# Weights' sums and subtractions at the start of a CIN tower: one operand from PSUM in place of two from SBUF

## The reference

```python
e = stack([tbl_f[ids[:, f]] for f in range(64)], axis=1)        # (512, 64, 16)
x, outs = e, []
for W, b in ((W0, b0), (W1, b1), (W2, b2)):                     # 128 outputs each
    z = einsum('bhd,bfd->bhfd', x, e).reshape(B, h * f, d)      # outer product of the fields
    x = einsum('oc,bcd->bod', W, z) + b[None, :, None]
    outs.append(x.sum(axis=2))
h = concatenate([concatenate(outs, axis=1), dense_ctx], axis=1)  # (512, 400)
y = relu(relu(h @ W_top1 + b_top1) @ W_top2 + b_top2) @ W_top3   # (512, 1)
```

## Time and profile before

| | |
|---|---|
| runs | 1191.19, 1192.84, 1193.23 us, median 1192.84 |
| profiled execution | 1193.48 us, of which the span 1191.7 us |
| PE busy | 1120.7 us (94%) |
| DVE busy | 1011.0 us (85%) |
| POOL busy | 989.1 us (83%) |
| ACT busy | 704.5 us (59%) |
| first matmul | at 49.06 us |

### The profile page before, as it was taken

The page is one execution under the profiler, slowest core; times in us unless marked ns, Lnnn a source line. Parts: engine busy times, 40 slices in busy tenths (PEclk is TensorE's granted clock), DMA queues, the critical chain, the costliest instruction groups (busy, mean ns, idle before and its releaser), DMA issues.

```text
span 1191.7 us, 13969 instructions
## 1 busy us (share of the span) xinstructions
PE 1120.7 (94%) x4212; PEld 758.3 (64%) x4212; DVE 1011.0 (85%) x685; ACT 704.5 (59%) x682; POOL 989.1 (83%) x419
## 2 busy tenths in 40 slices
PE   0379999999999999999999999999999999999998
PEld 0146666666666666666766666666666666667685
DVE  4478998989989999989898998999898889897542
ACT  2245566566666666675666666656666666665533
POOL 6669999999999999999999999999999997776000
PEclk9989999999999999999999999999999999999999
DMA  6552232525252515334252524252342525242991
GB/s 226 137 161 65 85 83 78 161 65 166 73 150 63 155 46 147 91 88 150 64 165 73 156 78 133 68 144 71 111 127 76 154 73 160 76 151 106 273 297 48
DMA packets 103835, 142.85 MB, mean 120 GB/s; under 512 B 11745, under 2 KB 55009, under 8 KB 103042
## 3 DMA queue, kind: packets, MB, share of 16 engines
q1 hardware_dynamic: 95618, 140.42, 39.1%
q0 software_dynamic: 8192, 2.11, 2.0%
HBM read 114.96 MB, written 27.53 MB: 120 GB/s over the span
## 4 chain that ended last, share of the span: by engine, by line
POOL 62%; PE 17%; issue 14%; DMA 4%; DVE 1%; SPq 1%; ACT 1%; POOLq 0%; ACTq 0%; DVEq 0%
POOL z_lo L509 46%; POOL emb L500 16%; PE acc L1015 9%; PE acc L1010 3%; DMA z<-gram_scratch 3%; PE turn_gram_ps L1079 1%; DMA land<-x_scratch 1%; PE z_ps L1141 1%; ACT z_hi L977 0%; DVE z_lo L754 0%; DVE z L577 0%; SPq L441 0%; SPq L369 0%; PE x0t_ps L1183 0%; PE turn_gram_ps L1183 0%
## 5 line engine op out<-in xcount | busy, mean ns | idle before, releaser
L509 POOL TENSOR_TENSOR z_lo<-z,z_hi 128x2048 fp32r<-128x2048 f32 x159 | 734.9, 4622 | 47.0 <-ACT z_hi L789 44.1
L1015 PE MATMUL acc<-z_hi,w_hi 128*128 128x512 f32 x960 | 412.4, 430 | 3.0 <-POOL z_lo L509 2.1
L789 ACT ACTIVATE z_hi<-z 128x2048 fp32r<-128x2048 f32 x160 | 306.3, 1914 | 181.4 <-PE acc L1015 170.4
L1015 PE MATMUL acc<-z_hi,w_lo 128*128 128x512 f32 x960 | 378.8, 395 | 0.0
L1015 PE MATMUL acc<-z_lo,w_hi 128*128 128x512 f32 x960 | 378.8, 395 | 0.0
L577 DVE TENSOR_TENSOR z<-operand_even,x_shift 128x2048 f32<-128x2048 f32 x144 | 328.5, 2282 | 31.8 <-DMA x_shift<-x_scratch 16.8
L500 POOL DMA_INDIRECT emb<-in_tables,rows_chunk x256 | 254.0, 992 | 62.0 <-issue 56.9
L1010 PE MATMUL acc<-z,w_sb 128*128 128x512 f32 x640 | 293.7, 602 | 0.6 <-ACT x L818 0.4
L589 DVE TENSOR_TENSOR z_lo<-z_ps,z_hi 128x1024 fp32r<-128x1024 f32 x160 | 194.5, 1215 | 71.0 <-ACT z_hi L798 71.0
L1015 PEld LDWEIGHTS acc<-z_hi,w_hi 128*128 128x128 f32 x960 | 180.8, 188 | 62.8 <-issue 18.9
L577 DVE TENSOR_TENSOR z<-operand_odd,x_shift 128x2048 f32<-128x2048 f32 x96 | 218.8, 2279 | 0.5 <-ACT operand_odd L765 0.3
(11 more groups left out here) (92 smaller groups left out, 454.2 us busy)
## 6 DMA issues: line engine op xcount, KB each, us to landing
land<-x_scratch SPq DMA_DIRECT2D x128, 256.0 KB
land<-x_scratch SPq DMA_DIRECT2D x128, 128.0 KB
x_shift<-x_scratch SPq DMA_DIRECT2D x16, 1024.0 KB, 5.8
gram_scratch<-gram SPq DMA_DIRECT2D x32, 512.0 KB, 4.3
x_shift<-x_scratch SPq DMA_DIRECT2D x16, 768.0 KB, 7.7
z<-gram_scratch SPq DMA_DIRECT2D x10, 1024.0 KB, 10.8
x_scratch<-emb SPq DMA_DIRECT2D x32, 192.0 KB, 2.9
x_shift<-gram_scratch SPq DMA_DIRECT2D x6, 1024.0 KB, 10.5
```

The costliest lines, as they stand in the source:

```text
L509: pool.tensor_tensor(z_lo[:, slot], z[:, Z_SLOT[pos]], z_hi[:, slot].bitcast(F32), ALU.subtract).then_inc(subtracted, 1)
L789: act.activation(z_hi[:, SPLIT_SLOT[pos]], z[:, Z_SLOT[pos]], ACT.Copy).then_inc(rounded, 1)
L1015: mm = pe.matmul(acc[:, :], w[:, tile, :], zz[:, slot, q, :], start=False, stop=stop and n == 2)
```

## The change

The layer 1 weights are added in pieces of 512 columns. ScalarE first copies each piece of the b half to a PSUM bank; VectorE adds the a half from SBUF and leaves the sum in the bank (split units) or writes it to `w0_sb` (plain unit). ScalarE rounds the pieces from the bank to w_hi, and VectorE subtracts w_hi (SBUF) from the bank (PSUM) to get w_lo. The 48 tiles of layer 2 go the same way in twelve pieces: ScalarE copies a piece to a bank and rounds it from SBUF, VectorE subtracts. Five banks are used in turn: two of z_ps, acc2, turn_gram_ps and x0t_ps. The waits of TensorE are for the last piece.

```diff
--- before.py
+++ after.py
@@ -73,6 +73,14 @@
 GRAM_BLOCKS = 2 * HALF_BLOCKS
 PLAIN_BLOCKS = W2_PART // F_BLOCK
 TOP1, TOP2 = 512, 256
+PIECE = COLS // HID
+L1_PIECES, SPLIT_PIECES = L1_SPLIT // PIECE, SPLIT_TILES // PIECE
+PLAIN_PIECES = (slice(0, COLS), slice(COLS, (L1_PLAIN + 1) * HID))
+
+
+def piece(weights, k):
+
+    return weights[:, k * PIECE:(k + 1) * PIECE, :].rearrange("p t o -> p (t o)")
 
 
 def is_plain(k):
@@ -212,6 +220,7 @@
         ids_sb = ids_sb.bitcast(I32)
         z_flat = z[:, :, :, :].rearrange("p a q n -> p (a q n)")
         w0b_split_stage = z_flat[:, 0:L1_SPLIT * HID].rearrange("p (t o) -> p t o", o=HID)
+        w0b_split_flat = z_flat[:, 0:L1_SPLIT * HID]
         w0b_stage = z_flat[:, L1_SPLIT * HID:(L1_SPLIT + L1_PLAIN + 1) * HID]
 
         wt1_sb, wt1d_sb = x0_shift[:, 0, 0:3, :], x0_shift[0:DENSE, 0, 3, :]
@@ -236,6 +245,12 @@
         z_ps = ps("z_ps", [P, 2, COLS])
         turn_gram_ps = ps("turn_gram_ps", [P, COLS])
         x0t_ps = ps("x0t_ps", [P, 2 * BLOCKS, FIELDS])
+        def stage_of(k):
+
+            return stage[k if k < L1_PIECES else (k - L1_PIECES) % len(stage)]
+
+        stage = [z_ps[:, 0, :], z_ps[:, 1, :], acc2[:, :], turn_gram_ps[:, :],
+                 x0t_ps[:, :, :].rearrange("p b f -> p (b f)")]
 
 
         ids_in, const_in, w0_in, w1_in, w1_split_in, top_in = (sem(s) for s in ("ids_in", "const_in", "w0_in", "w1_in", "w1_split_in", "top_in"))
@@ -244,6 +259,7 @@
         w2_rounded, w2_split = sem("w2_rounded"), sem("w2_split")
         gram_rounded, gram_split = sem("gram_rounded"), sem("gram_split")
         w_rounded, w_split = sem("w_rounded"), sem("w_split")
+        w0_staged = sem("w0_staged")
         rows_step, rows_ready, rows_free, rows_copied, gather_begun = (
             sem(s) for s in ("rows_step", "rows_ready", "rows_free", "rows_copied", "gather_begun"))
         w0_summed = sem("w0_summed")
@@ -546,22 +562,20 @@
                 dve.wait_ge(rows_step, step + 3)
                 dve.tensor_scalar(rows[:, cols], ids_tmp[:, cols], info_sb[:, 2:3], None, ALU.add).then_inc(rows_ready, 1)
 
-            dve.wait_ge(w0_in, 64)
             w0_flat = w0_sb[:, :, :].rearrange("p t o -> p (t o)")
-            dve.tensor_tensor(w_whole[:, 0:L1_SPLIT, :], w_whole[:, 0:L1_SPLIT, :], w0b_split_stage, ALU.add).then_inc(w0_summed, 1)
-            dve.tensor_tensor(w0_flat, w0_flat, w0b_stage, ALU.add).then_inc(w0_summed, 1)
-
-            def split_weights(step, tiles):
-
-                dve.wait_ge(w_rounded, step)
-                dve.tensor_tensor(w_lo[:, tiles, :], w_whole[:, tiles, :], w_hi[:, tiles, :].bitcast(F32),
+            for k in range(L1_PIECES):
+                dve.wait_ge(w0_staged, k + 1)
+                dve.tensor_tensor(stage[k], piece(w_whole, k), stage[k], ALU.add).then_inc(w0_summed, 1)
+            for k, cols in enumerate(PLAIN_PIECES):
+                bank = stage[L1_PIECES + k][:, 0:cols.stop - cols.start]
+                dve.wait_ge(w0_staged, L1_PIECES + k + 1)
+                dve.tensor_tensor(w0_flat[:, cols], w0_flat[:, cols], bank, ALU.add).then_inc(w0_summed, 1)
+            for k in range(SPLIT_PIECES):
+                dve.wait_ge(w_rounded, k + 1)
+                dve.tensor_tensor(piece(w_lo, k), stage_of(k), piece(w_hi, k).bitcast(F32),
                                   ALU.subtract).then_inc(w_split, 1)
-
-            split_weights(1, slice(0, L1_SPLIT))
-            split_weights(2, slice(L1_SPLIT, SPLIT_TILES))
             dve.wait_ge(const_in, 48)
             dve.tensor_scalar(bias3_sb[:, :], bias_sb[:, 2:3], float(EMBED), None, ALU.mult).then_inc(bias3_ready, 1)
-            dve.wait_ge(w0_summed, 2)
 
             def times(bank, tiles, x0_tiles):
                 return operand[bank][:, :].rearrange("p (q n) -> p q n", q=1).to_broadcast([P, tiles, COLS]), x0_tiles
@@ -886,10 +900,23 @@
             g0, g1 = layer1_group(c0), layer1_group(c1)
             take_rows(c0)
             take_rows(c1)
-            act.wait_ge(w0_summed, 1)
-            act.activation(w_hi[:, 0:L1_SPLIT, :], w_whole[:, 0:L1_SPLIT, :], ACT.Copy).then_inc(w_rounded, 1)
+            act.wait_ge(w0_in, 64)
+            for k in range(L1_PIECES):
+                act.activation(stage[k], w0b_split_flat[:, k * COLS:(k + 1) * COLS], ACT.Copy).then_inc(w0_staged, 1)
+            for k, cols in enumerate(PLAIN_PIECES):
+                act.activation(stage[L1_PIECES + k][:, 0:cols.stop - cols.start], w0b_stage[:, cols], ACT.Copy).then_inc(w0_staged, 1)
+            for k in range(L1_PIECES):
+                act.wait_ge(w0_summed, k + 1)
+                act.activation(piece(w_hi, k), stage[k], ACT.Copy).then_inc(w_rounded, 1)
             act.wait_ge(w1_split_in, 16)
-            act.activation(w_hi[:, L1_SPLIT:, :], w_whole[:, L1_SPLIT:, :], ACT.Copy).then_inc(w_rounded, 1)
+            for k in range(L1_PIECES, SPLIT_PIECES):
+                before = k - L1_PIECES
+                if L1_PIECES <= before < len(stage):
+                    act.wait_ge(w0_summed, before + 1)
+                else:
+                    act.wait_ge(w_split, before + 1 if before < L1_PIECES else k - len(stage) + 1)
+                act.activation(stage_of(k), piece(w_whole, k), ACT.Copy)
+                act.activation(piece(w_hi, k), piece(w_whole, k), ACT.Copy).then_inc(w_rounded, 1)
 
             to_bank(g0, 0, 0)
             to_bank(g0, 1, 1)
@@ -1099,12 +1126,12 @@
                 gram_of(prev, 3)
 
             c0 = Chunk(0, 0)
-            pe.wait_ge(w0_summed, 2)
-            pe.wait_ge(w_split, 1)
+            pe.wait_ge(w0_summed, L1_PIECES + len(PLAIN_PIECES))
+            pe.wait_ge(w_split, L1_PIECES)
             layer1(c0)
             layer1(c0.plus(1))
             pe.wait_ge(w1_in, 16)
-            pe.wait_ge(w_split, 2)
+            pe.wait_ge(w_split, SPLIT_PIECES)
             pe.wait_ge(const_in, 48)
             for i in range(L2_GROUPS):
                 layer2(c0, i, range(QUAD))
```

## The result

The changed kernel takes 1185.7 us (median of 4 runs, 1184.82 to 1185.84), the kernel before 1192.77 us: 7.1 us less, ratio 0.9941 (95% interval 0.9925 to 0.9957). Run again beside three of the experiments it took 1185.23 us against 1193.94, ratio 0.9928 (0.9915 to 0.9942). The profiled execution of 1185.75 us has a span of 1183.9 us, 7.8 less than before. The forecast was 1184.8 us, range 1182.8 to 1187.4.

The account below looks back on a forecast made before the run. TensorE sets the pace after a start bounded by 32 serial gathers on GpSimd. Span 1191.70 - 8.01 of removed stalls = 1183.69 us, other terms 0; as execution 1185.47, less 0.64 to the median: 1184.8 us, range 1182.8 to 1187.4.

Parts of the forecast that it names:

- What bounds the start: Before TensorE's two starts: a chain of 32 gathers on GpSimd, one after the other, at a pitch of 1.25 us.
- the sum's first term: Time is the start of TensorE (49.06 us), plus fixed work, plus the tail; the change touches only the start.
- The removed holds: Chunk 0's gathers: three long ones beside the replaced VectorE instructions lose 1.06, 0.80 and 6.15 us of stall, 8.01 in all.
- The sums: Layer 1 weight additions, SBUF first and PSUM second: hold no gather (0) or give back 1.06 us; taken as 0.
- ScalarE's cost: Added copies and roundings: 24 x 0.60 = 14.4 us, ending at 32.4 us (bounds 29.9 and 43.7), covered.
- VectorE's cost: 20 pieces of about 0.70 us, done at about 33.1 us, ahead of the need; cost 0.
- Moved rigidly: Chunk 0's stores and loads meet the same company and shift unchanged; TensorE asks for weights at 41.05 us at the earliest.
- L689's hold: Chunk 1's last gather, held 1.47 us by unchanged L689: stays; bounds of change -1.47 to +1.0 us, taken as 0.
- A: Rival: one operand in PSUM holds GpSimd's gathers as well; 3.2 us slower, 1196.0 us; chance 0.03.
- B: Rival: the long gathers have another cause than VectorE, for instance weights' traffic, and stay; 1192.8 us; chance 0.03.
- C: Rival: L689 comes behind chunk 1's last gather, so that stall goes too; 1183.3 us; chance 0.20.
- D: Rival: only part arrives (sums hold, L689's worst phase or late chunk 1 loads), 2 to 5 us: 1186.8 to 1189.8; chance 0.12.

Follow-up runs that it names:

- late chunk 0: The changed kernel with two more 2048-column roundings on ScalarE (3.8 us, results unused) ahead of the first group's first rounding: 1183.27 us, ratio 0.9915.
- x1's early copy: The changed kernel with the copy of chunk 0's x1 out of the accumulator moved three instructions forward on ScalarE: 1185.48 us, ratio 0.9931.
- the pieces alone: The kernel before with sums, roundings and subtractions cut into 512-column pieces, every operand still in SBUF, no copies to PSUM: 1186.48 us, ratio 0.9942.
- the first unit by PSUM: The changed kernel with the first group's unit 1 also through PSUM, so L703 (L689 before) is gone: 1183.93 us, ratio 0.9921.

## Why the prediction was right

*What bounds the start.* The chain of gathers is right. The last gather of chunk 1 moved by 54.71 - 46.76 = 7.95 us, TensorE's second start by 7.89, the span by 7.8. The late chunk 0 shows it from the other side. But the sum's first term, "the start of TensorE", is not what carries the gain on. x1's early copy moved TensorE's second start by 2.95 us and the time by nothing; what carries it is GpSimd's first low part of chunk 1. In the change both moved by 7.89 us, so the wrong term gave the right number.

*The removed holds, 8.01 us.* Right in size, gather by gather. The reason was right in its first half (a VectorE instruction with two SBUF operands holds a gather to its end) and too wide in its second: I spoke of PSUM as what frees the gather. The holds were large because the instructions were long (6.56 us in one), and cutting alone takes away 7.49 of the 8.01. The prediction had the row for it: the gather at 12.81 us, not held by an instruction 0.43 us behind its start. I read it as a detail of the last term. It says that an instruction which begins after the gather's first moments doesn't hold it; the experiments added that the next one in the queue doesn't renew a hold, so that it costs no more than one instruction's length.

*The sums, 0 to 1.06 us, taken as 0.* Right: with SBUF first and PSUM second the gather at 10.56 us takes 0.95.

*ScalarE's cost.* Covered, as forecast. The size was off: 12.58 us for 24 instructions, 0.52 each, where I had 0.60. Single copies are recorded with about 0.60 us, but they start 0.52 us apart, so in a row their records overlap; the cheaper bound from the 1536-column rounding (0.49) was the nearer one. It ended at 30.49 us and not at 32.4, 3.35 us ahead of the next copy. (The two bounds of the end come out at 29.8 and 43.8 us, not 29.9 and 43.7.)

*VectorE's cost.* 0.69 us a piece (0.70 estimated), done at 31.21 us, covered.

*Moved rigidly.* Only nearly. From the store of x0 to the first matmul it took 49.06 - 34.55 = 14.51 us before and 39.89 - 26.77 = 13.12 after. So chunk 0 came 1.16 us earlier than forecast (41.05). By itself it cost and gave nothing, since chunk 0 isn't on the path; but it moved L689 against the gathers.

*L689's hold, -1.47 to +1.0, taken as 0.* Right by size (1.48), but it is another gather: the thirty-first instead of the thirty-second, because chunk 0's chain moved by 9.2 us and the gathers by 8.0. The size came out the same because the phase did, 0.68 us (43.07 - 42.39) for 0.70. That is luck: the two chains moved apart by 9.2 - 7.95 = 1.25 us, just one gather with its pause. In other kernels of the table this hold was 0.94 to 2.11 us, or it was gone. The bound of +1.0 was too wide: the worst phase met, 0.06 us ahead of the gather, cost 0.6 us more than 1.47.

*The rivals.* A and B are out by the changed kernel's trace itself. C did not come by itself in the changed kernel (in the trace of the pieces alone it did) and was made twice (the first unit by PSUM, chunk 0 later): 1183.9 and 1183.3 us, forecast 1183.3. Of D nothing is in the trace up to the second start; from there to the end the shift shrinks from 7.89 to about 7.7 us. The forecast and the result differ by 0.9 us, and the kernel before alone gives medians of 1192.77 to 1193.94 in different comparisons, so the measurement leaves nothing that could be explained.

## What to carry to other kernels

An indirect gather that GpSimd issues can be held by a VectorE instruction with two SBUF operands that began before it and still runs about 0.1 us after its start, until that instruction ends. If gathers are on the path, look in the timeline for long ones beside such instructions, and first cut these into short pieces (512 columns here); moving an operand to PSUM takes the small rest and costs copies. When an engine starts earlier and the time doesn't move, look for a distance that stays the same in every trace: what it starts from is what sets the time. And ask of each chain at the start how much it has to spare: here useless work in one chain made the kernel faster, because it moved one instruction out of the other's way.

## What was not expected of the hardware

- The hold isn't renewed by the next VectorE instruction in the queue: twelve back to back (7.48 us) cost the gathers 0.35 us, one of 6.56 us cost 6.15. How little twelve cost is partly their phase.
- Reading two operands from SBUF and writing to PSUM holds a gather as well (1.58 us for 0.95), so the reads do it.
- A gather holds VectorE too, by little: pieces with two SBUF operands that begin within 0.01 us of a gather's start take 0.72 or 0.73 us in place of 0.69, one that began 0.04 us before took 0.77; pieces with one such operand stay at 0.68 to 0.70.
- Behind 7.18 us of idle time in TensorE the first pair of matmuls took 2.04 us, at a granted clock of 0.50; behind 0.87 us of idle time it took 1.09, at 1.00. The time did not depend on it.
